# Latent attention of a fused kernel: head pairs through one ring of two-bank slots, and mask and maximum of a head in one VectorE instruction

## The reference, cut to what matters

```python
H, D = (16, 64); R = C // 8; ROPE = D // 2; NOPE = D - ROPE          # C = 128
q = (x @ Wq).reshape(b, t, H, D).transpose(0, 2, 1, 3)
ckv = x @ Wkva
kv_latent, k_rope = (ckv[:, :, :R], ckv[:, :, R:])
kv = (kv_latent @ Wkvb).reshape(b, t, H, NOPE).transpose(0, 2, 1, 3)
q = jnp.concatenate([q_nope, _rope(q_rope)], axis=-1)
k = jnp.concatenate([kv, _rope(k_rope)], axis=-1)
v = jnp.concatenate([kv, jnp.zeros_like(k_rope)], axis=-1)
att = jnp.einsum('bhqd,bhkd->bhqk', q, k) / jnp.sqrt(jnp.float32(D))
att = jnp.where(jnp.tril(jnp.ones((t, t), dtype=bool)), att, -jnp.inf)
y = jnp.einsum('bhqk,bhkd->bqhd', jax.nn.softmax(att, axis=-1), v)
return y.transpose(0, 2, 1, 3).reshape(b, t, H * D) @ Wo
```

## Time and profile before

| | |
|---|---|
| runs | 1943.57, 1953.51, 1965.15 us |
| span of the profiled execution, first to last instruction | 1926.2 us |
| what the median has beyond that span | 27.3 us |
| TensorE busy in the whole span | 1542.9 us (80%) |
| the latent stage, 1140 to 1557 us | 417 us: TensorE 379.1, VectorE 127.6, ScalarE 128.5, GpSimd 111.3 us busy |
| mean granted TensorE clock in that stage | 0.87 of 2.4 GHz |

### The profile page before, as it was taken

How to read it: one execution, slowest core, us unless ns; L and a number is a source line. 1 busy time by engine, 2 the same in 40 slices (tenths; PEclk the granted TensorE clock), 3 DMA queues, 4 the chain that set the end, 5 groups by cost and what they waited for, 6 DMA issues and landing times. The chain is left out here.

```text
span 1926.2 us, 24318 instructions
## 1 busy us (share of the span) xinstructions
PE 1542.9 (80%) x9156; PEld 783.5 (41%) x9158; DVE 998.0 (52%) x1384; ACT 708.8 (37%) x1306; POOL 576.9 (30%) x602
## 2 busy tenths in 40 slices
PE   5778738899689996985579857999999857779982
PEld 3355513333334443432244334444454432245541
DVE  3799556778332326763367523333342135568855
ACT  2435224667410003762237532333332222255521
POOL 1478523543111103310024124223311110037650
PEclk7799966899889997996669868999896679979985
DMA  3000010000100001000100010000000000000000
GB/s 94 1 1 1 1 40 1 1 1 2 70 1 0 0 0 46 1 1 8 43 3 1 1 40 1 1 1 1 1 1 1 1 26 0 6 1 2 2 3 22
DMA packets 19153, 20.58 MB, mean 11 GB/s; under 512 B 9803, under 2 KB 15163, under 8 KB 18408
## 3 DMA queue, kind: packets, MB, share of 16 engines
q1 hardware_dynamic: 19048, 19.13, 3.3%
HBM read 17.94 MB, written 1.05 MB: 10 GB/s over the span
## 5 line engine op out<-in xcount | busy, mean ns | idle before, releaser
L1677 DVE TENSOR_REDUCE L2f_nm<-P 128x2 f32<-128x768 f32 (+3 forms) x88 | 99.0, 1126 | 222.4 <-PE P L1582 222.0
L1593 PE MATMUL P<-L2f_qs,L2f_ks 49*128 49x256 f32 (+3 forms) x512 | 148.2, 512 | 17.1 <-DMA L2f_qs<-L2f_mt 17.1
L1652 ACT ACTIVATE L2f_prob<-P 128x512 f32<-128x512 f32 x160 | 89.8, 597 | 188.1 <-PE P L1593 188.1
L997 DVE TENSOR_REDUCE L0f_nm<-P 128x2 f32<-128x768 f32 (+3 forms) x88 | 97.4, 1119 | 53.2 <-PE P L904 53.2
L2160 PE MATMUL P<-L0m_hm,L0m_w 128*128 128x512 f32 x256 | 112.5, 599 | 2.7 <-POOL L0m_hm L2122 2.6
L1509 POOL TENSOR_SCALAR_AFFINE_SELECT L2f_prob<-L2f_prob 128x512 f32<-128x512 f32 x64 | 39.6, 637 | 247.6 <-ACT L2f_prob L1652 247.5
L1593 PEld LDWEIGHTS P<-L2f_qs,L2f_ks 49*128 49x128 f32 x512 | 82.1, 212 | 73.1 <-issue 41.4
L1579 PE MATMUL P<-L2f_ks,L2f_qs 48*128 48x512 f32 (+3 forms) x512 | 107.7, 498 | 0.0
L953 ACT ACTIVATE L0f_prob<-P 128x512 f32<-128x512 f32 x160 | 87.1, 604 | 36.7 <-PE P L915 35.3
L2463 POOL TENSOR_TENSOR L3x_exm<-L3x_exm,L3x_rec 128x2048 f32<-128x2048 f32 x16 | 72.4, 4529 | 26.1 <-DVE L3x_rec L2637 26.1
L2160 PEld LDWEIGHTS P<-L0m_hm,L0m_w 128*128 128x128 f32 x256 | 49.1, 192 | 65.0 <-issue 62.9
(11 more groups left out here) (583 smaller groups left out, 3371.9 us busy)
## 6 DMA issues: line engine op xcount, KB each, us to landing
L0m_w<-in_L0m_w SPq DMA_DIRECT2D x1, 2048.0 KB, 7.9
L0f_va<-in_L0f_va SPq DMA_DIRECT2D x3, 512.0 KB, 4.7
in_xt<-in_x SPq DMA_DIRECT2D x1, 1024.0 KB
L0x_segi<-in_segb SPq DMA_DIRECT2D x1, 1024.0 KB, 5.0
L0m_w<-in_L0m_w SPq DMA_DIRECT2D x1, 1024.0 KB, 9.9
L2f_qs<-L2f_mt SPq DMA_DIRECT2D x64, 2.0 KB, 1.7
out<-out_o SPq DMA_DIRECT2D x4, 256.0 KB, 2.5
L1x_va<-in_va SPq DMA_DIRECT2D x3, 256.0 KB, 3.1
```

The lines of the kernel that those rows point to most:

```text
L997: nc.vector.tensor_reduce(S.nm[:, qt, first:first + 2 * many].rearrange("p (i e) -> p e i", e=2), P[:, bank:bank + 2, 0:many * width].rear ...
L1593: m = mm(P[:, bank, at:at + width], S.ks[b % 2][64 * e:64 * e + 49, kt * 128:(kt + 1) * 128], S.qs[b % 2][64 * e:64 * e + 49, pair, q0:q0 ...
L1652: nc.scalar.activation(S.group_prob(b, g)[:, slot, :], P[:, bank, :], ACT.Exp).then_inc(*S.act_done.up())
L1677: nc.vector.tensor_reduce(S.nm[:, qt, first:first + 2 * many].rearrange("p (i e) -> p e i", e=2), P[:, bank:bank + 2, 0:many * width].rear ...
```

## The change

Class `LatentPairs` takes the place of `LatentHeads`, with another table of steps, and an unused older version of the stage is deleted.

- The three pairs of banks 0-1, 2-3 and 4-5 are one ring of two-bank slots for `k`, `p`, `t1`, the rounds and A, B, C; `lat`, `t2` (the `w` step) and `out` take turns in bank 7; the values stay in bank 6. A slot's fourth next use waits for its reader.
- A step A, B or C covers an even and an odd head: 10 in a half in place of 20, and ScalarE takes one exponential of 1024 columns over both banks. `p` and `t1` are doubled likewise.
- The rounds lose the mask matmuls. VectorE does a two-stream instruction for each head and query block (`tensor_tensor_reduce`): it adds a bf16 mask row tile, zero but for the last 128 columns, writes the sum back to PSUM, and takes the maximum.
- ScalarE negates the maxima when it copies them; two DMAs of four rows each replace the eight of one row.

```diff
-    RING = ("k", "lat", "p", "t1", "t2", "A", "B", "C", "out")
-    BY_DVE = ("k", "out")
+    DOUBLE = ("k", "p", "t1", "round", "A", "B", "C")
+    SINGLE = ("lat", "t2", "out")
+    BY_DVE = ("k", "round", "out")
+    SLOTS = 3
...
+    def slot_for(self, pe, step):
+        n = self.place[step]
+        if n > self.SLOTS:
+            pe.wait_ge(*self.gone(self.double[n - 1 - self.SLOTS]))
+        return 2 * ((n - 1) % self.SLOTS)
...
-STEP_latent_order = """w0 R1 R0 la R2 t0 A0 p0 A1 B0 A2 B2 sa0 lb R4 lc R5 A4 sb0 lt A3 sc0 ka R6 A6 C0 A7 B4 t1 R8 p1 rec B6 B1 C2 turn ma R7 sa1 A5 B3 p2 t2 t3 mb mc R3 kb B5 x0 B7 x1 sb1 C1 mt R9 kl sc1 R10 C3 res out p3""".split()
+STEP_latent_order = """w R0 la R1 lb lc t0 R2 lt uA0 R3 uA1 sa ka uB0 R4 uB1 sb kl p0 uC R5 sc rec vA0 ma R6 vA1 sd turn mb vB0 x0 R7 mc mt
+ vB1 se t1 R8 p1 x1 vC R9 sf out res R10""".split()
...
-                    sp.wait_ge(S.act_done.sem, max([S.freed[step]] + [S.freed["t1", b, 4 * half + n] for n in range(4)]))
-                    for h in range(8):
-                        row = 64 * (h % 2) + 48
-                        sp.dma_start(S.qs[b % 2][row:row + 1, 4 * half + h // 2, :], S.mt[half][h:h + 1, :])\
+                    sp.wait_ge(S.act_done.sem, max(S.freed[step], S.freed["t1", b, 2 * half], S.freed["t1", b, 2 * half + 1]))
+                    for e in range(2):
+                        sp.dma_start(S.qs[b % 2][64 * e + 48:64 * e + 49, 4 * half:4 * half + 4, :], S.mt[half][e:8:2, :])\
...
                             mm(P[:, bank + e, p * width:(p + 1) * width], S.qs[b % 2][64 * e:64 * e + 48, pair, qt * 128:(qt + 1) * 128],
-                               S.ks[b % 2][64 * e:64 * e + 48, 0:width], start=p == 0, stop=False)
-                    for e in range(2):
-                        m = mm(P[:, bank + e, 0:many * width].rearrange("p (h k) -> p h k", k=width)[:, :, width - 128:width],
-                               G["identb"][:], mask[:].unsqueeze(1).to_broadcast([128, many, 128]), start=False, stop=True)
-                    m.then_inc(*S.s_full.up())
+                               S.ks[b % 2][64 * e:64 * e + 48, 0:width], start=True, stop=True)
+                    m.then_inc(*S.full.up())
                 elif kind in S.EXPS:
...
+                    tiles = ([(2 * g + i, 0, 0, 0, T)] if kind == "A" else
+                             [(2 * g + i, 1, 0, 128, 384), (2 * g + i, 3, 384, 384, 128)] if kind == "B" else
+                             [(2 * g + x, 2, 256 * x, 256, 256) for x in range(2)])
+                    for pair, kt, at, q0, width in tiles:
+                        for e in range(2):
+                            m = mm(P[:, bank + e, at:at + width], S.ks[b % 2][64 * e:64 * e + 49, kt * 128:(kt + 1) * 128],
+                                   S.qs[b % 2][64 * e:64 * e + 49, pair, q0:q0 + width], start=True, stop=True)
...
-                    nc.vector.tensor_reduce(S.nm[:, qt, first:first + 2 * many].rearrange("p (i e) -> p e i", e=2),
-                                            P[:, bank:bank + 2, 0:many * width].rearrange("p e (i k) -> p e i k", k=width),
-                                            AX.X, ALU.max, negate=True).then_inc(*S.s_free.up())
+                    for p in range(many):
+                        for e in range(2):
+                            at = P[:, bank + e, p * width:(p + 1) * width]
+                            m = nc.vector.tensor_tensor_reduce(out=at, in0=at, in1=mask[:, T - width:T], scale=1.0, scalar=-3.0e38,
+                                                               op0=ALU.add, op1=ALU.max,
+                                                               accum_out=S.nm[:, qt, first + 2 * p + e:first + 2 * p + e + 1])
+                    m.then_inc(*S.dve_done.up())
```

More of the change, by code:

```diff
@@ new lines, in bank_of, with rounds_of, units_of, prob_of @@
+    def bank_of(self, eng, step):
+        eng.wait_ge(self.one_full.sem, self.place[step])
+        return 7
+    def rounds_of(self, b, half):
+        return max(self.freed[r] for r in self.freed if r[0] == "round" and r[1] == b and r[2][0] == half)
+    def units_of(self, b, g, part):
+        return max(self.freed[part, b, (g, i)] for i in range(1 if part == "C" else 2))
+    def prob_of(self, b, g):
+        return self.prob[(4 * b + g) % 3]
+STEP_latent_order = """w R0 la R1 lb lc t0 R2 lt uA0 R3 uA1 sa ka uB0 R4 uB1 sb kl p0 uC R5 sc rec vA0 ma R6 vA1 sd turn mb vB0 x0 R7 mc mt
+ vB1 se t1 R8 p1 x1 vC R9 sf out res R10""".split()
@@ L1433, in one @@
             return (name, b - 1, 0) if half == 0 and b else None
+        if name == "w":
+            return ("t2", b, half)
         if name[0] == "t":
[L1435 to L1446, removed]
+            return ("t1", b + 1, 2 * half + n) if b + 1 < NB else None
+        if name in ("ka", "kl"):
+            return ("lat" if name == "kl" else "k", b + 1, 0) if half == 0 and b + 1 < NB else None
+        return (name[0], b + 2, 2 * half + n) if b + 2 < NB else None
+    project = lambda b: [s for qt in range(QT) for s in (("p", b, qt), ("x", b, qt))]
+    order = [("k", 0, 0), ("lat", 0, 0)] + project(0) + [("t1", 0, 0), ("t1", 0, 1)]
+    order += spread_between(project(1) + [("t1", 0, 2), ("t1", 0, 3)], rounds(0))
     for h in range(2 * NB):
@@ L1565, in _ @@
                 elif kind == "round":
-                    half, qt, i = n
-                    if S.first["round", b, half] == s:
-                        pe.wait_ge(S.act_done.sem, max(S.freed["t1", b, 4 * half + x] for x in range(4)))
+                    half, qt, i, many, width = shape_of(s)
+                    if S.leads["round", b, half] == s:
+                        pe.wait_ge(S.act_done.sem, max(S.freed["t1", b, 2 * half], S.freed["t1", b, 2 * half + 1]))
                         pe.wait_ge(S.k_ready.sem, b + 1)
-                    use = S.place[s]
@@ new lines, in _ @@
+                    nc.vector.tensor_tensor(k[:], P[:, bank, :], ck[:], ALU.mult)
+                    link(dve, nc.vector.tensor_tensor(S.kr[:], P[:, bank + 1, :], sk[:], ALU.mult), S.dve_done)
+                    nc.vector.scalar_tensor_tensor(out=k[:], in0=S.kr[:], scalar=one[:, 0:1], in1=k[:], op0=ALU.add,
+                                                   op1=ALU.add).then_inc(*S.k_ready.up())
+                elif kind == "round":
+                    half, qt, i, many, width = shape_of(s)
+                    bank = S.slot_of(dve, s)
+                    if S.leads["round", b, half] == s and b:
+                        dve.wait_ge(S.one_full.sem, S.place["t2", b - 1, half])
+                    first = 8 * half + 2 * many * i
+                    for p in range(many):
[5 more added lines that the diff above has]
+                    m.then_inc(*S.dve_done.up())
```

558 lines of the change are left out of this document (124 added, 434 removed).

## The result

The changed kernel takes 1816.74 us (median of four runs, 1814.64 to 1818.55); the kernel before, run beside it, 1949.09 us (1943.57 to 1965.15). The ratio is 0.9356, 95% interval 0.9318 to 0.9393: 6.4% faster by that ratio, 132 us (6.8%) between the medians, where 1896.5 us was forecast with a range from 1855 to 1938. The direction was right, and the gain is more than twice the forecast.

The account below looks back on a forecast made before the run. TensorE's list of work was taken to bound the latent stage. Terms -40 - 23 - 14 + 12 + 6 + 2 summed to -57 us, a span of 1869 and a median of 1896.5 us, 8-in-10 range 1855 to 1938.

Parts of the forecast that it names:

- the share of either level as it is: TensorE in the latent stage: time split between 2.4 and 1.2 GHz assumed unchanged, so the clock got no term.
- the clock comes back: Rival, latent stage: the half-clock stretch from 1460 to 1532 us stays away, some 35 us more gained, 1862 us; chance 0.13.
- A second HAM failure mode: psum-queue depth-cycling: Rival, latent stage: short idles at `w` and in the ring lower TensorE's clock, about 1993 us at three halves; chance 0.10.
- The median is 27.3 above that span, and I keep that distance: Whole kernel: 27.3 us between profiled span and median run kept, turning a forecast span of 1869 into 1896.5 us.
- A, B, C in pairs: TensorE's A, B, C steps: alternating heads cover 107.7 us in place of 148.2, -40 us, bounds -52 to -30.
- Masks: TensorE's rounds: mask matmuls leave, -23 us over eight halves, from -17 to -30.
- Rows: TensorE's waits for the DMAs' rows of maxima: -14 of 17.1 us, from -8 to -17.
- `w`: TensorE's `w` step waits for VectorE's pass over R10's maxima in seven passages: +12 us, from +8 to +17.
- Ring: PSUM slots in the latent stage: R0 to R2's VectorE passes don't quite fit, uA1 waits; +6 us, from 0 to +15.
- The +2 for the first half's rounds: First half, rounds without A, B, C between go at VectorE's pace, 18.5 for 12.4 us: +2 us, from 0 to +6.
- VectorE's pass: VectorE's two-stream instruction: 279 ns for 128 columns, 691 for 512, 90 ns write; 18.5 us a half, from 15.5 to 21.5.
- VectorE as the bound: Rival, latent stage: passes take 1546 ns for 512 columns, about 43 us a half, gain about 20 us, 1933 us; chance 0.09.

Follow-up runs that it names:

- rows covered: Kernel before with lb, R4 and lc moved ahead of a half's first A, single heads and eight DMAs kept: 1898.41 us, ratio 0.9774.
- alternating: Kernel before with only its step table reordered, A, B, C of even and odd heads next to each other: 1904.73 us, ratio 0.9817.
- alternating and covered with two DMAs: Kernel before with even and odd heads' A, B, C adjacent, lb, R4, lc ahead of the first A, and two four-row DMAs: 1858.93 us, ratio 0.9611.
- alternating and covered: Kernel before with even and odd heads' A, B, C adjacent and lb, R4, lc ahead of the first A, eight DMAs kept: 1866.33 us, ratio 0.9598.

## Why the prediction was wrong

Three of the kernels lead in four steps from before to the change, and their medians give each part. The medians come from different groups, and the runs of before in these differ, 1940 to 1967 us in median, so the first step is the least certain; the lengths of the stage in the profiles stand beside them:

| step | us | difference | stage in the profiles | forecast |
|---|---|---|---|---|
| before, to two DMAs for the rows | 1949.1 to 1873.7 | -75 | 429.1 to 376.9, -52 | -14 |
| to pairs, ring and new table, masks on TensorE, `w` covered | 1828.0 | -46 | 326.6, -50 | -40 + 6 + 2 = -32 |
| to masks on VectorE | 1799.2 | -29 | 299.3, -27 | -23 |
| to `w` right behind R10, as the change has it | 1816.7 | +18 | 318.7, +19 | +12 |

**The step that failed is the clock.** The prediction said that it leaves "the share of either level as it is", since "TensorE's idle stretches move from the DMA's wait to `w`, and are about as long in sum". Their sum is about the same, 18.7 us before and 18.2 after (the earlier trace rows and the waits above), and the clock is not. The wait's 15 us were forecast as 14; with them went 37 us of TensorE's busy time in the profiled run, the price of matmuls at 1.2 GHz. Two kernels show it that leave every matmul as it is and take these waits away in different ways: fewer DMAs (14.9 us of waits, 37.3 of busy time) and order (10.9 of idle time, 29.5 of busy time). In both the clock is 1.00 from 1206 us to the last half. For the whole change an estimate from the stage's lengths and mean clocks (429.1 us at 0.86, 318.7 at 0.92) is some 120 and 51 us at 1.2 GHz; were TensorE busy in all of it, half would be lost, 60 and 25: about 35 of the 110 us. The rival "the clock comes back" had this outcome with 35 us and a chance of 0.13, but for a wrong reason: it looked to the pairs, not to the wait that stands right ahead of the fall. That wait was in the timeline to be read; I had looked at the half clock's stretch and not at what TensorE did just before it. The prediction's "gap of 1 us at A0" was also read from the one half of the earlier trace rows: the eight waits there were 2.5, 1.4, 2.2, 1.0, 1.1, 1.4, 2.1 and 5.4 us.

The Trainium skill, "TensorE: Matmul & The Clock Gate", section "HAM oscillation — how this bites in real kernels", describes such a loss in a kernel whose matmuls wait for DMAs again and again. The trace agrees in that: without 14.9 of the 17.1 us of waits for the rows' DMAs the same matmuls take 37 us less. The section's waits are some 3 to 5 us long; here waits of 1.1 to 2.5 us had a fall behind them, and for this kernel the trace decides. The rival that rested on the same page's section "A second HAM failure mode: psum-queue depth-cycling" did not come: by that rule the ring would have lost clock, and with the ring and no wait at `w` the clock was 1.00 for 210 us.

**The second failure is the distance to the median.** "The median is 27.3 above that span, and I keep that distance": the runs that came with spans all have 1.6 to 1.8 us between span and time. So the profile before was of a run of some 1928 us, 21 below the median of 1949.1. Its mean clock over the whole span is 0.849; in the group of the two-DMA kernel, the kernel before has 0.848 at 1927.60 us and lower clocks in all its longer runs. This gives the rest: 109 us between the profiled spans, 132 between the medians.

Point by point:

- *A, B, C in pairs*, -40 for a forecast cover of 100 to 115 us: it is 84.5, which is 80 steps at the 1.06 us that the earlier trace rows show at full clock. The lower end of the term, 96 us, took that price at the old mean clock. The price was right, the clock was not. In the step from single heads with two DMAs to pairs in the new ring, where both kernels keep their clock (0.94 and 0.95), the row falls from 129.1 to 89.1, the 40 us of the term.
- *Masks*, -23: 28.9 without the wait at `w`, 18.9 with it, the forecast between them, both within its bounds of 17 to 30. Part of the difference is that VectorE's passes lengthen the wait at `w` and the ring's.
- *Rows*, -14 of waits: 16.3 in the change.
- *`w`*, +12 with waits of 10 to 17 us: 14.2 us of waits for the 13 of the sum, in eight passages rather than seven; the first half has one too. In time it is 17.6, since three of the waits are followed by a lower clock; this is the same failed step, in small.
- *Ring*, +6: 2.6 us of waits. The +2 for the first half's rounds was not measured by itself.
- *VectorE's pass*: 325 and 718 ns for 279 and 691, the write 140 for 90. In all (118.4 + 35.9) / 8 = 19.3 us in a half for 18.5, between the bounds of 15.5 and 21.5. VectorE as the bound did not come; nor did a loss by half clock, though the small falls behind `w` are its beginning.

**What stays open** is which waits are followed by a fall, and how long a fall lasts. In the kernel before, waits of 2.5, 1.1 and 2.1 us are followed by one, and waits of 2.2 and 1.4 us are not; five of the eight waits at `w`, of 1.5 to 1.95 us, are not either. And the kernel before has one short fall, at 1230 us, with no wait ahead of it, like the one at 1490 us with two DMAs:

```profile
1206.00:1230.00 24.00, 24.00 (x137) 12.46 (x136) 8.30 (x9) 10.05 (x20) 7.03 (x9) 1.00 0.00 1
1230.00:1234.00 4.00, 4.00 (x16) 2.10 (x16) 1.23 (x1) 1.45 (x3) 0.64 (x1) 0.68 0.00 0
```

So the waits are shown as the cause of the loss in sum, and not of each single fall. Behind waits of 0.9 to 4.5 us the clock was low for 3 to 14 us (the changed kernel; before with two DMAs; two falls of before), some 27 us (rows covered; alternating; alternating and covered with two DMAs), 34 us (alternating and covered) or 58 us (before, 1457 to 1515 us), with TensorE busy nearly all the time. The kernels with the new ring all came back within some 7 us of such a wait; why they do was not settled.

## What to carry to other kernels

Where a profile shows a stretch at half clock, look at what TensorE did in the few microseconds ahead of it: waits of 1 to 2 us there can cost several times their length, in this stage 52 us for 15. A kernel with those waits taken away and every matmul left as it is tells whether they are the cause. Cover such waits first, by fewer DMAs or by independent matmuls in front of them, and price the other parts of a change at the clock that is then there. A transpose or any step that waits for the last result of another engine belongs behind the next independent work: here three words in a table, `R0 la w`, gave 17.6 us more.

## What the hardware showed that I had not expected

- Two heads on the two row halves run beside each other also when four matmul instructions of one precede four of the other: 1.14 us for a step B, against 1.06 in alternating order and some 2.1 (estimate) for two lone heads one after the other.
- The 128x1 accumulator write behind VectorE's two-stream reduction takes 140 ns, but a pass of 512 columns starts some 0.65 us after the one before it (718 + 140 ns by their rows), so the two overlap.
- The kernel before, whose clock falls at several places behind short waits, spread over 60 us from run to run in one group (1923.68 to 1984.33); the same kernel with two DMAs, 1.00 from 1190 to 1466 us, over 2 us.
- A fall of the clock behind a wait of 2.1 us lasted 58 us, with TensorE busy for all of the 56 us from 1458 to 1514.
